# Summing a graph layer's messages by rounds of four blocks, with eleven picked tiles in each slot

## The chip, the core and the metric

The kernel runs on one core of a Trainium2 chip. The metric is the time of one execution on the device, in microseconds (us). TensorE is the matrix engine, VectorE, ScalarE and GpSimd the three others, SyncE issues most DMAs.

## What is computed

A graph of 12500 nodes with 16 values each and 400000 edges sorted by target, with 8 features each. After a normalisation and a ReLU come three layers of edge-conditioned convolution, then a product with a 16x16 matrix, and the result is added to x.

```python
def _nnconv(x, src, dst, edge_attr, ew, eb, rw, rb):
    W = (edge_attr @ ew + eb).reshape(edge_attr.shape[0], x.shape[1], rw.shape[1])
    xj = x[src]
    msg = jnp.einsum('ei,eio->eo', xj, W)
    agg = jax.ops.segment_sum(msg, dst, num_segments=x.shape[0])
    return agg + x @ rw + rb
# layers 1 and 2: h = relu(batchnorm(_nnconv(h, ...))); layer 3: relu(_nnconv(h, ...)) @ pred_w + pred_b
```

## The kernel before

**Tiling.** A tile is 128 edges, one in each partition. Five tiles make a block (640 edges that follow each other in the sorted order), five blocks a slot: 25 tiles, 3200 edges. A layer has G = 125 slots; five slots are a body, whose buffers turn (SLOTS). All three layers run the same code, so there are 375 slots.

**Getting x[src].** GpSimd fetches 15 of the 25 tiles of a slot from a table of the nodes in HBM, one indirect DMA for a tile (L469, `gather`). The other 10 are picked on chip. ScalarE makes one-hot matrices of the low nine bits of the source, as 4 x 128 rows, in two halves of five tiles: four `distance` (L915) and four `low_hot` (L921) in each half, from keys that SyncE loads as a broadcast (L396). TensorE multiplies each tile's one-hots with the node values, which are split in an upper and a lower part: 4 x 2 matmuls of 400 columns a tile (L1076, `pick`), into one of four PSUM banks. VectorE takes each bank with the mask of the upper bits (L684, `take_picks`), and after each half reduces its tiles to 16 values an edge (L689).

**Products and sums.** VectorE multiplies the 16 values with the 8 features (L639, once for the picked tiles and once for the fetched ones), ScalarE copies the 16 values beside them (L931, L937): 144 columns an edge, in one of three parts of `xbig`. TensorE sums them by target: `sum_tiles` (L1043) runs over j and then over the five blocks, and multiplies each tile with a one-hot of 32 targets (`hot`, L631, two buffers). Each block writes its own 32 partitions of PSUM, the column group n % 4, with n the number of the block. Four blocks form a round, so rounds don't end where slots do; a slot completes one round, every fourth slot two. ScalarE copies a completed round (`copy_rounds`, L879), TensorE transposes and merges it with a shifted one-hot (`transpose_round`, L1090, L1091), ScalarE copies that (L887, L888), and for each quad of four slots TensorE makes messages (`messages_of`, L1101, L1103), which VectorE adds into `agg` (`add_quad`, L725, five additions).

**Order.** Every engine has its own written order, joined by semaphores. TensorE, in slot g: the ten picks of slot g+1, with the transpositions of the rounds ended in slot g-1 after the second and the fourth and a quad's messages after the eighth, then the sum of slot g. VectorE, in slot g: products, round one-hots, feature copy for g+1 (L734), takes and reduction of the first half of g+1, target one-hots (L631), takes and reduction of the second half, masks for g+2 (L670), and, behind every fourth slot, the additions. ScalarE: the row copies, copies of the transposed rounds, then the two halves' one-hots of g+2, with the copy of the completed round between distances and one-hots of the second half. A tile may be picked once its bank was taken, four tiles before. A part of `xbig` is written again after slot k-3 is summed, a `hot` after k-2.

**Opening.** Sources of picked tiles come from HBM in two loads of ScalarE's queue (L838) into `key_all`, tiles across, 20 bytes a piece; VectorE splits them (L535 to L538), TensorE transposes the keys (L991), and ScalarE writes them to HBM (L850), from where the broadcasts read. The targets are loaded half by SyncE and half by ScalarE (L843). `rows` holds the node values of a layer in a tensor of its own, `rows_room`.

## Time and profile before

| what | value |
|---|---|
| median of 3 runs | 7477.99 us (7477.64 to 7480.97) |
| profiled execution: time, span | 7481.76 us, 7478.8 us |
| mean granted TensorE clock | 0.977 |
| busy: TensorE, VectorE, ScalarE, GpSimd | 7244.2, 5851.7, 4981.2, 5326.7 us |
| picking matmuls, L1076 | 30000 of 348 ns |
| gathers, L469 | 5625 of 947 ns |

The profile is one execution, recorded by the hardware. Busy time of an engine counts no waiting and no issuing. PE is TensorE's matmuls and PEld its weight loads, DVE VectorE, ACT ScalarE, POOL GpSimd, SP SyncE. Matmuls overlap, so the mean duration of one is longer than the distance from one to the next. "Idle before" is the time that the engine stood still ahead of an instruction, with what ended it.

### The profile page before, as it was taken

The page shows a single profiled execution, that of the slowest core. Times are in us where ns is not written, and L with a number is a line of the kernel's source. Part 1 is how long each engine was busy: PE and PEld are TensorE (multiplying, and loading weights), DVE is VectorE, ACT ScalarE, POOL GpSimd, SP SyncE. Part 2 cuts the span into 40 slices and gives each one's busy share as a digit, 9 for nine tenths or more (in the row PEclk, how much of TensorE's full clock was granted, in tenths as well). Part 3 has the DMA queues.
Part 4 walks back from the last instruction along what each step waited for, and adds up shares of the span by engine and source line. Part 5 has one row for each costly group of instructions (what it writes and reads, how often), then busy time and mean ns, then how long its engine had stood idle before and what let it go on. Part 6 is the DMA issues. An engine that isn't in the chain of part 4 may idle for free.

```text
span 7478.8 us, 138584 instructions
## 1 busy us (share of the span) xinstructions
PE 7244.2 (97%) x53192; PEld 6608.9 (88%) x53192; DVE 5851.7 (78%) x7566; ACT 4981.2 (67%) x8367; POOL 5326.7 (71%) x5635
## 2 busy tenths in 40 slices
PE   4999999999999999999999999999999999999998
PEld 1999999999999699999999999968999999999998
DVE  3888878787878678788888888867888888787885
ACT  3666666666666566666666666656666666666665
POOL 4677777777777377777777777737777777777772
PEclk7999999999999799999999999979999999999998
DMA  8111111111111111111111111111111111111110
GB/s 39 29 31 31 31 31 31 31 31 30 30 31 31 27 29 31 31 31 31 31 31 31 31 31 31 31 26 30 31 31 30 32 29 31 31 31 31 31 31 21
DMA packets 783276, 229.34 MB, mean 31 GB/s; under 512 B 643869, under 2 KB 733869, under 8 KB 782619
## 3 DMA queue, kind: packets, MB, share of 16 engines
q1 hardware_dynamic: 529252, 172.27, 11.0%
q0 software_dynamic: 180000, 46.44, 7.3%
q10 hardware_dynamic: 73367, 1.76, 1.0%
q8 instruction: 425, 6.96, 0.4%
q14 instruction: 232, 1.90, 0.1%
HBM read 216.52 MB, written 3.52 MB: 29 GB/s over the span
## 4 chain that ended last, share of the span: by engine, by line
PE 85%; DVE 7%; issue 4%; DVEq 3%; DMA 1%; ACT 0%; ACTq 0%
PE bank L1076 68%; PE bank L1043 10%; DVE xbig L639 3%; DVEq L720 3%; PE bank L1032 2%; PE bank L1091 1%; DVE agg L725 1%; DVE spread L684 1%; PE bank L1090 1%; PE bank L1101 1%; PE bank L1103 1%; DMA key_all<-in_src 1%; PE bank L1148 1%; PE bank L1160 1%; DVE xg L689 0%
## 5 line engine op out<-in xcount | busy, mean ns | idle before, releaser
L469 POOL DMA_INDIRECT xg<-node_table,idx x5625 | 5325.9, 947 | 2036.1 <-issue 1766.2
L1076 PE MATMUL bank<-nodes,low_hot 128*128 128x400 f32 x30000 | 5742.7, 348 | 68.9 <-DVE spread L684 52.2
L1076 PEld LDWEIGHTS bank<-nodes,low_hot 128*128 128x128 f32 x30000 | 5403.8, 188 | 279.0 <-issue 180.9
L915 ACT ACTIVATE distance<-key_all,low_id 128x640 bf16<-128x640 int16 x3000 | 2242.9, 818 | 1912.7 <-issue 1219.7
L684 DVE TENSOR_TENSOR spread<-mask,bank 128x400 f32<-128x400 uint8 x3750 | 1989.0, 564 | 1234.7 <-PE bank L1076 1234.5
L921 ACT ACTIVATE low_hot<-distance,one 128x640 fp32r<-128x640 bf16 x3000 | 2232.9, 817 | 0.0
L689 DVE TENSOR_REDUCE xg<-spread 128x80 f32<-128x2000 f32 x750 | 1677.0, 2236 | 25.7
L639 DVE TENSOR_TENSOR xbig<-xg,bank 128x1280 f32<-128x1280 f32 x750 | 1327.3, 1810 | 1.0 <-issue 0.2
L1043 PE MATMUL bank<-xbig,hot 128*32 128x144 f32 x18750 | 994.5, 295 | 0.0
L1043 PEld LDWEIGHTS bank<-xbig,hot 128*32 128x32 f32 x18750 | 820.6, 109 | 162.0 <-issue 99.1
L631 DVE TENSOR_TENSOR hot<-bank,dst_rel 128x800 f32<-128x800 f32 x375 | 367.8, 981 | 0.0
L887 ACT ACTIVATE zT<-bank 128x100 f32<-128x100 f32 x471 | 112.8, 239 | 225.5 <-PE bank L1091 223.7
L725 DVE TENSOR_TENSOR agg<-agg,bank 16x100 f32 x471 | 118.5, 252 | 140.2 <-issue 69.0
L1090 PEld LDWEIGHTS bank<-merge,z 128*128 128x128 f32 x942 | 167.2, 188 | 59.1 <-issue 54.9
L1090 PE MATMUL bank<-merge,z 128*128 128x100 f32 x942 | 177.0, 269 | 28.5 <-DVE agg L725 22.0
L931 ACT ACTIVATE xbig<-xg 128x160 f32<-128x160 f32 x375 | 126.6, 338 | 65.5 <-ACT low_hot L921 65.5
L1091 PE MATMUL bank<-merge,z 128*16 128x100 f32 x942 | 162.5, 254 | 0.0
L879 ACT ACTIVATE z<-bank 128x144 f32<-128x144 f32 x471 | 117.7, 270 | 58.2 <-PE bank L1043 58.2
L670 DVE TENSOR_TENSOR mask<-bank,fine 128x250 uint8<-128x250 f32 x375 | 153.6, 410 | 0.0
L937 ACT ACTIVATE xbig<-xg 128x240 f32<-128x240 f32 x375 | 145.6, 388 | 0.0
L714 DVE TENSOR_SCALAR merge<-bank,slide 128x100 f32<-128x100 f32 x471 | 139.0, 312 | 0.0
L734 DVE COPY bank<-ea 128x200 f32<-128x200 f32 x375 | 133.1, 355 | 0.3 <-DVE agg L593 0.2
(109 smaller groups left out, 998.6 us busy)
## 6 DMA issues: line engine op xcount, KB each, us to landing
key_all<-edge_keys SPq DMA_DIRECT2D x375, 320.0 KB, 3.7
xg<-node_table,idx POOLq DMA_INDIRECT x5625
ea<-in_edge_attr SPq DMA_DIRECT2D x375, 100.0 KB
idx<-in_src SPq DMA_DIRECT2D x375, 7.5 KB
node_table<-rows_room SPq DMA_DIRECT2D x3, 781.2 KB
xbig<-node_table SPq DMA_DIRECT2D x9, 192.0 KB
xbig<-in_x SPq DMA_DIRECT2D x2, 781.2 KB
xbig<-in_dst ACTq DMA_DIRECT2D x1, 782.5 KB, 67.4
```

The costliest lines, as they stand in the source:

```text
L469: pool.indirect_dma_start(out=xg[u][:, j, :], out_offset=None, in_=table[:, :], in_offset=bass.IndirectOffsetOnAxis(ap=idx[u][:, j:j + 1], ...
L631: return nc.vector.tensor_tensor(buf, p_col[:, 0:wide].unsqueeze(1).to_broadcast([P, tiles, wide]), rel.unsqueeze(2).to_broadcast([P, tile ...
L639: return nc.vector.tensor_tensor(buf[:, :, D:D + FD].rearrange("p j (f d) -> p j f d", d=D), xj, ef, ALU.mult)
L684: nc.vector.tensor_tensor(spread[:, t - t0, :, :], mask[k % PAIR][:, t, :].unsqueeze(1).to_broadcast([P, D, FINE]), p_sel[t % BANKS].rearr ...
L689: nc.vector.tensor_reduce(xg[u % SLOTS][:, FETCHED + t0:FETCHED + t1, :], spread[:, 0:t1 - t0, :, :], AX_X, ALU.add).then_inc(s_xg, 1)
L720: bases = [dve.value_load(base_i[0:1, r:r + 1], min_val=0, max_val=N - 1) for r in rounds]
L915: nc.scalar.activation(distance[f][:, 0:tiles.stop - tiles.start, :], key[u % KEYS][:, tiles, :], ACT.Abs, bias=low_id[:, f:f + 1]).then_i ...
L921: nc.scalar.activation(low_hot[:, f, tiles, :], distance[f][:, 0:tiles.stop - tiles.start, :], ACT.Relu, bias=one[:], scale=-1.0).then_inc ...
L1043: done = nc.tensor.matmul(p_z[n // GANG % PAIR][c * WIN:(c + 1) * WIN, :], onehots[:, t, :], buf[:, t, :], start=j == 0, stop=j == RUN - 1)
L1076: last = nc.tensor.matmul(p_sel[t % BANKS], low_hot[:, f, t, :], nodes[i][:, f, :, :].rearrange("p d f -> p (d f)"), start=(f, i) == (0, 1 ...
L1090: nc.tensor.matmul(p_zT, z[r % PAIR][:, D:D + FD], merge[r % SHIFTS][:], start=True, stop=True)
L1091: nc.tensor.matmul(p_zxT, z[r % PAIR][:, 0:D], merge[r % SHIFTS][:], start=True, stop=True).then_inc(s_T, 1)
```

## The change

`sum_tiles`, which summed the five blocks of a slot, becomes `sum_round`, which sums the four blocks of a round, for each round that a slot completes; a block left over is summed in the next slot's round, from the slot before's buffers. So `xbig` and `hot` are released by rounds (`slot_summed`), and there are three `hot` buffers. `rows_room` goes; `rows` lies in the third part of `xbig`. Every slot picks 11 tiles and fetches 14: the halves have five and six tiles, keys, one-hots, masks and `spread` grow accordingly, and the PSUM bank of a tile goes by a running count. The picked sources are loaded as one DMA of 125 contiguous rows of 1920 integers, one row a slot; keys are cut from them in place, and the upper bits are transposed instead. The diff, cut to its core:

```diff
-PICKED = 10
-FETCHED = TILES - PICKED
+MOST = 11
+FETCHED = 15
 FOLD = 4
 FOLD_BITS = 2
 BANKS = 4
 SLOTS = 5
 PAIR = 2
+HOTS = 3
...
-PARTS = (slice(0, 5), slice(5, 10))
-HALF = 5
+HALF = 6
...
-        rows_room = sb("rows_room", [P, PER * D])
-        rows = rows_room[0:NODE_P, :].rearrange("p (m d) -> p m d", d=D)
         xbig = sb("xbig", [P, TRIPLE * TILES * WIDTH])
+        rows_at = (TRIPLE - 1) * TILES * WIDTH
+        rows = xbig[0:NODE_P, rows_at:rows_at + PER * D].rearrange("p (m d) -> p m d", d=D)
...
-        hot = [sb(f"hot{i}", [P, TILES, WIN]) for i in range(PAIR)]
+        hot = [sb(f"hot{i}", [P, TILES, WIN]) for i in range(HOTS)]
...
+        src_c = xbig[0:G, src_at:src_at + LATER].bitcast(I32)
+        src_int = spread[0:G, :, :, :].rearrange("p a b c -> p (a b c)")[:, 0:LATER].bitcast(I32)
+        fine_f = spread[0:G, :, :, :].rearrange("p a b c -> p (a b c)")[:, 0:MOST * P].rearrange("g (c p) -> g c p", p=P)
...
+        def picks_of(g):
+
+            return MOST
+
+        def parts_of(g):
+
+            return slice(0, RUN), slice(RUN, picks_of(g))
+
+        def picks_to(k):
+
+            return MOST + sum(picks_of(h % G) for h in range(k))
+
+        def slot_summed(eng, k):
+
+            if k >= 0:
+                eng.wait_ge(s_round, k // G * R + rounds_done(k % G))
...
-                        for j in range(FETCHED):
+                        for j in range(TILES - picks_of(b * SLOTS + u)):
...
-            dve.wait_ge(s_src, 32)
-            step(nc.vector.tensor_scalar(src_int, src_pick, 7 + FOLD_BITS, None, ALU.logical_shift_right))
-            step(nc.vector.tensor_copy(fine[:].rearrange("p (g j) -> p g j", g=G), src_int))
-            step(nc.vector.tensor_scalar(src_int, src_pick, P * FOLD - 1, None, ALU.bitwise_and))
-            nc.vector.tensor_copy(key_f, src_int).then_inc(s_keyf, 1)
-            for c in range(PICKED):
-                dve.wait_ge(s_keyT, c + 1)
-                nc.vector.tensor_copy(key16[:, c, :], bank[c % 2][0:G, 0:P]).then_inc(s_key16, 1)
+            dve.wait_ge(s_src, 16)
+            step(nc.vector.tensor_scalar(src_int, src_c, P * FOLD - 1, None, ALU.bitwise_and))
+            for to, part in zip(picked_to(key16), picked_from(src_int)):
+                last = nc.vector.tensor_copy(to, part)
+            last.then_inc(s_key16, 1)
+            step(nc.vector.tensor_scalar(src_c, src_c, 7 + FOLD_BITS, None, ALU.logical_shift_right))
+            for to, part in zip(picked_to(fine_f), picked_from(src_c)):
+                last = nc.vector.tensor_copy(to, part)
+            last.then_inc(s_finef, 1)
+            fine_c = fine[:].rearrange("p (g c) -> p c g", c=MOST)
+            for c in range(MOST):
+                dve.wait_ge(s_fineT, c + 1)
+                nc.vector.tensor_copy(fine_c[:, c, :], bank[c % 2][:, 0:G]).then_inc(s_fine, 1)
...
-                dve.wait_ge(s_seg, k + CREDIT - 1)
+                slot_summed(dve, k - 2)
                 n = (b * SLOTS + u) * BLOCKS
-                onehots(hot[k % PAIR][:], dst_rel[:, n:n + BLOCKS, :].rearrange("p n j -> p (n j)")).then_inc(s_hot, 1)
+                onehots(hot[k % HOTS][:], dst_rel[:, n:n + BLOCKS, :].rearrange("p n j -> p (n j)")).then_inc(s_hot, 1)
...
             def take_picks(layer, b, u, half):
 
 
                 k = layer * G + b * SLOTS + u
-                t0, t1 = PARTS[half].start, PARTS[half].stop
+                g = b * SLOTS + u
+                t0, t1 = parts_of(g)[half].start, parts_of(g)[half].stop
+                done, at = picks_to(k), TILES - picks_of(g)
                 dve.wait_ge(s_mask, k + 1)
                 dve.wait_ge(s_xg, k * 2 + half)
                 for t in range(t0, t1):
-                    dve.wait_ge(s_pick, k * PICKED + t + (1 + PICKED))
+                    dve.wait_ge(s_pick, done + t + 1)
                     nc.vector.tensor_tensor(
                         spread[:, t - t0, :, :],
                         mask[k % PAIR][:, t, :].unsqueeze(1).to_broadcast([P, D, FINE]),
-                        p_sel[t % BANKS].rearrange("p (d f) -> p d f", d=D), ALU.mult).then_inc(s_taken, 1)
-                dve.wait_ge(s_taken, k * PICKED + (t1 + PICKED))
-                nc.vector.tensor_reduce(xg[u % SLOTS][:, FETCHED + t0:FETCHED + t1, :],
+                        p_sel[(done + t) % BANKS].rearrange("p (d f) -> p d f", d=D), ALU.mult).then_inc(s_taken, 1)
+                dve.wait_ge(s_taken, done + t1)
+                nc.vector.tensor_reduce(xg[u % SLOTS][:, at + t0:at + t1, :],
                                         spread[:, 0:t1 - t0, :, :], AX_X, ALU.add).then_inc(s_xg, 1)
...
-                dve.wait_ge(s_seg, k + CREDIT - 2)
-                products(xw[k % TRIPLE][:, TAKEN, :], xg[u][:, TAKEN, :], p_ea[k % PAIR][:, TAKEN, :])
+                slot_summed(dve, k - 2)
+                taken = slice(TILES - picks_of(b * SLOTS + u), TILES)
+                products(xw[k % TRIPLE][:, taken, :], xg[u][:, taken, :], p_ea[k % PAIR][:, taken, :])
...
-            for i in range(PICKED // RUN):
-                act.dma_start(src_pick[:, :, i * RUN:(i + 1) * RUN],
-                              src_b.rearrange("(g a) p j -> a p g j", a=BLOCKS)[FETCHED // RUN + i, :, :, :]
-                              ).then_inc(s_src, 16)
+            act.dma_start(src_c, src.rearrange("(g e) -> g e", g=G)[:, GE - LATER:GE]).then_inc(s_src, 16)
...
-                    act.wait_ge(s_key16, PICKED)
-                    act.dma_start(keys.rearrange("(c q) p -> q c p", q=G), key16).then_inc(s_keyd, 16)
+                    act.wait_ge(s_key16, 1)
+                    act.dma_start(keys.rearrange("(g c) p -> g c p", g=G), key16).then_inc(s_keyd, 16)
...
-                    act.wait_ge(s_seg, layer * G + g + (1 + CREDIT))
+                    act.wait_ge(s_round, n + 1)
...
-            def sum_tiles(g, buf, onehots):
-
-
+            def sum_round(layer, r):
+
+                n = layer * R + r
+                if n >= PAIR:
+                    pe.wait_ge(s_z, n - PAIR + 1)
+                blocks = range(r * GANG, min((r + 1) * GANG, NB))
                 for j in range(RUN):
-                    for a in range(BLOCKS):
-                        n, t = g * BLOCKS + a, a * RUN + j
-                        c = n % GANG
-                        done = nc.tensor.matmul(p_z[n // GANG % PAIR][c * WIN:(c + 1) * WIN, :], onehots[:, t, :],
-                                                buf[:, t, :], start=j == 0, stop=j == RUN - 1)
-                return done
+                    for i in blocks:
+                        k, t, c = layer * G + i // BLOCKS, i % BLOCKS * RUN + j, i % GANG
+                        last = nc.tensor.matmul(p_z[r % PAIR][c * WIN:(c + 1) * WIN, :], hot[k % HOTS][:, t, :],
+                                                xw[k % TRIPLE][:, t, :], start=j == 0, stop=j == RUN - 1)
+                last.then_inc(s_round, 1)
...
-                before = t - BANKS if t >= BANKS else max(range(t, PICKED, BANKS)) - PICKED
-                pe.wait_ge(s_taken, k * PICKED + (before + 1 + PICKED))
+                n = picks_to(k) + t
+                pe.wait_ge(s_taken, n - BANKS + 1)
                 for f in range(FOLD):
                     for i in (1, 0):
                         last = nc.tensor.matmul(
-                            p_sel[t % BANKS], low_hot[:, f, t, :],
+                            p_sel[n % BANKS], low_hot[:, f, t, :],
...
-                        behind = layer * R + ((g + 1) * BLOCKS - 1) // GANG - 1
-                        if behind > 0:
-                            pe.wait_ge(s_z, behind)
-                        sum_tiles(g, xw[k % TRIPLE], hot[k % PAIR]).then_inc(s_seg, 1)
+                        for r in rounds_of(g):
+                            sum_round(layer, r)
...
```

## Rows read from the trace of the kernel before

**Rows 1.** Page, part 1: busy us of each engine, share of the span, instructions.
```profile
PE 7244.2 (97%) x53192; PEld 6608.9 (88%) x53192; DVE 5851.7 (78%) x7566; ACT 4981.2 (67%) x8367; POOL 5326.7 (71%) x5635
```

**Rows 2.** Page, part 4: the chain that ended last, by line.
```profile
PE bank L1076 68%; PE bank L1043 10%; DVE xbig L639 3%; DVEq L720 3%; PE bank L1032 2%; PE bank L1091 1%; DVE agg L725 1%; DVE spread L684 1%; PE bank L1090 1%; PE bank L1101 1%; PE bank L1103 1%; DMA key_all<-in_src 1%; PE bank L1148 1%; PE bank L1160 1%; DVE xg L689 0%
```

**Rows 3.** Groups, whole run: line engine op out<-in shapes xcount | busy us, mean ns | idle before.
```profile
L1076 PE MATMUL bank<-nodes,low_hot 128*128 128x400 f32 x30000 | 5742.7, 348 | 68.9 <-DVE spread L684 52.2 <-DVE nodes L652 15.1 <-DVE agg L593 1.1
L469 POOL DMA_INDIRECT xg<-node_table,idx x5625 | 5325.9, 947 | 2036.1 <-issue 1766.2 <-DMA node_table<-rows_room 198.7 <-DMA ea<-in_edge_attr 71.2
...
L689 DVE TENSOR_REDUCE xg<-spread 128x80 f32<-128x2000 f32 x750 | 1677.0, 2236 | 25.7
L1043 PE MATMUL bank<-xbig,hot 128*32 128x144 f32 x18750 | 994.5, 295 | 0.0
```

**Rows 4.** Waits, whole run: engine line waited for: us in total, times, longest us.
```profile
PE bank L1076 <- DVE spread L684: 52.2, 92, 1.7
PE bank L1090 <- DVE agg L725: 22.0, 90, 0.6
...
POOL xg L469 <- issue: 1766.2, 5529, 77.2
```

**Rows 5.** Windows, a period of each kind: us, busy of each engine, PEclk, DMA, GB/s.
```profile
1334.45:1353.67 19.22, 18.50 (x135) 16.95 (x134) 15.99 (x23) 12.81 (x21) 14.35 (x17) 1.00 0.19 31
1353.67:1371.69 18.02, 18.02 (x136) 17.10 (x135) 14.81 (x18) 12.82 (x21) 13.28 (x15) 1.00 0.19 32
1371.69:1389.69 18.00, 18.00 (x135) 17.08 (x134) 15.05 (x19) 12.82 (x21) 13.74 (x15) 1.00 0.19 33
1389.69:1409.71 20.02, 20.02 (x159) 17.92 (x158) 14.81 (x18) 13.37 (x24) 15.15 (x17) 1.00 0.18 30
```

**Rows 6.** Timeline 1500:1525, kind 1: start us, us, engine line op out<-in xcount.
```profile
1504.50 2.64 PE L1043 MATMUL bank<-xbig,hot 128*32 128x144 f32 x50
...
1511.65 1.52 DVE L684 TENSOR_TENSOR spread<-mask,bank 128x400 f32<-128x400 uint8 x3
```

**Rows 7.** Timeline of TensorE, 1371.6:1390, kind 2.
```profile
1371.69 2.64 PE L1043 MATMUL bank<-xbig,hot 128*32 128x144 f32 x50
...
1377.27 0.36 PE L1090 MATMUL bank<-merge,z 128*128 128x100 f32 x2
...
1377.84 11.93 PE L1076 MATMUL bank<-nodes,low_hot 128*128 128x400 f32 x64
```

**Rows 8.** The same from 1371.6 to 1371.99: what of the sum had started.
```profile
1371.69 0.60 PE L1043 MATMUL bank<-xbig,hot 128*32 128x144 f32 x12
```

**Rows 9.** Timeline of VectorE, 1371.6:1390, kind 2.
```profile
1379.07 1.52 DVE L684 TENSOR_TENSOR spread<-mask,bank 128x400 f32<-128x400 uint8 x3
```

**Rows 10.** Timelines of VectorE and TensorE, 1334:1356, kind 0.
```profile
1338.45 1.79 DVE L725 TENSOR_TENSOR agg<-agg,bank 16x100 f32 x5 [0.72 <-issue]
...
1344.13 1.99 DVE L684 TENSOR_TENSOR spread<-mask,bank 128x400 f32<-128x400 uint8 x4
...
1340.38 0.43 PE L1090 MATMUL bank<-merge,z 128*128 128x100 f32 x2 [0.18 <-DVE agg L725]
...
1344.73 9.01 PE L1076 MATMUL bank<-nodes,low_hot 128*128 128x400 f32 x48 [0.54 <-DVE spread L684]
```

**Rows 11.** Timeline of ScalarE, 1334:1356, kind 0.
```profile
1334.61 2.98 ACT L915 ACTIVATE distance<-key_all,low_id 128x640 bf16<-128x640 int16 x4 [2.76 <-PE bank L1076]
1337.50 0.27 ACT L879 ACTIVATE z<-bank 128x144 f32<-128x144 f32 x1
```

**Rows 12.** The opening: timeline of VectorE, DMA of 0:95 (KB each, us to landing).
```profile
12.94 1.82 DVE L518 TENSOR_REDUCE ln_m<-xbig 125x100 f32<-125x1600 f32 x1 [7.80 <-DMA xbig<-in_x]
...
91.46 1.79 DVE L545 CAST xbig<-xbig 128x3125 f32<-128x3125 int32 x1 [34.00 <-DMA xbig<-in_dst]
...
DMA packets 132507, 5.63 MB, mean 59 GB/s; under 512 B 132083, under 2 KB 132256, under 8 KB 132506
...
key_all<-in_src ACTq DMA_DIRECT2D x2, 312.5 KB, 37.5
```

More of the change, by code:

```diff
@@ L62, in gnn_kernel @@
     assert E == G * GE and G == BODIES * SLOTS and FD == P and D * (F + 1) <= 512
[L63 removed]
+    assert GANG * WIN == P and QROUNDS * SPAN <= 512 and FETCHED % RUN == 0 and NB == BLOCKS * G
     assert N == NODE_P * PER and PER == CHUNKS * SUB and CHUNKS % SLOTS == 0 and CN <= 512
@@ L70, in gnn_kernel @@
     table = nc.dram_tensor("node_table", [N, D], F32, kind="Internal").ap()
-    keys = nc.dram_tensor("edge_keys", [G * PICKED, P], I16, kind="Internal").ap()
+    keys = nc.dram_tensor("edge_keys", [G * MOST, P], I16, kind="Internal").ap()
     def blocks_of(a, tail=""):
@@ L111, in gnn_kernel @@
         one = sb("one", [P, 1])
-        fine = sb("fine", [P, G * PICKED], U8)
-        mask = [sb(f"mask{i}", [P, PICKED, FINE], U8) for i in range(PAIR)]
+        fine = sb("fine", [P, G * MOST], U8)
+        mask = [sb(f"mask{i}", [P, MOST, FINE], U8) for i in range(PAIR)]
         spread = sb("spread", [P, HALF, D, FINE])
@@ L326, in landed @@
         def landed(eng, layer, g):
-            eng.wait_ge(s_gath[g % SLOTS], (layer * BODIES + g // SLOTS + 1) * 16 * FETCHED)
+            eng.wait_ge(s_gath[g % SLOTS], 16 * sum(TILES - picks_of(h % G) for h in
+                                                    range(g % SLOTS, layer * G + g + 1, SLOTS)))
         def ends_quad(g):
@@ L396, in load_keys @@
                 sp.dma_start(
-                    key[u % KEYS][:].rearrange("p t e -> p (t e)"),
-                    keys[bass.ds((b * SLOTS + u) * PICKED, PICKED), :].rearrange("(a t) e -> a (t e)", a=1)
-                    .to_broadcast([P, PICKED * P])).then_inc(s_key[u], 16)
+                    key[u % KEYS][:, 0:picks_of(g), :].rearrange("p t e -> p (t e)"),
+                    keys[(g + 1) * MOST - picks_of(g):(g + 1) * MOST, :].rearrange("(a t) e -> a (t e)", a=1)
+                    .to_broadcast([P, picks_of(g) * P])).then_inc(s_key[u], 16)
             AHEAD = 2
@@ L494, in _ @@
                 dve.sem_inc(s_low, 1)
-            for _ in range(PICKED):
+            for _ in range(MOST):
                 dve.sem_inc(s_taken, 1)
@@ L904, in compare_keys @@
                 k = layer * G + b * SLOTS + u
+                g = b * SLOTS + u
                 u = u % SLOTS
-                tiles = PARTS[half]
+                tiles = parts_of(g)[half]
                 act.wait_ge(s_key[u], body * 16 + 16)
-                act.wait_ge(s_pick, k * PICKED + tiles.stop)
+                if k:
+                    act.wait_ge(s_pick, picks_to(k - 1) + min(tiles.stop, picks_of((k - 1) % G)))
                 before = k * (4 * FOLD) + half * 2 * FOLD
@@ L978, in _ @@
         def _(pe):
-            for _ in range(PICKED):
+            for _ in range(MOST):
                 pe.sem_inc(s_pick, 1)
@@ L982, in _ @@
                 pe.sem_inc(s_root, 1)
-                pe.sem_inc(s_seg, 1)
             pe.wait_ge(s_ident, 1)
-            pe.wait_ge(s_keyf, 1)
-            flat = key_f.rearrange("p g j -> p (g j)")
-            for c in range(PICKED):
+            pe.wait_ge(s_finef, 1)
+            for c in range(MOST):
                 if c >= 2:
-                    pe.wait_ge(s_key16, c - 1)
-                nc.tensor.transpose(bank[c % 2][0:G, 0:P], flat[:, c * G:(c + 1) * G], ident[:]).then_inc(s_keyT, 1)
+                    pe.wait_ge(s_fine, c - 1)
+                nc.tensor.transpose(bank[c % 2][:, 0:G], fine_f[:, c, :], ident[0:G, 0:G]).then_inc(s_fineT, 1)
             def find_bases():
-                pe.wait_ge(s_key16, PICKED)
+                pe.wait_ge(s_fine, MOST)
                 pe.wait_ge(s_base, 1)
@@ L1067, in pick @@
                 k = layer * G + b * SLOTS + u
-                for half, tiles in enumerate(PARTS):
+                for half, tiles in enumerate(parts_of((b * SLOTS + u) % G)):
                     if t == tiles.start:
                         pe.wait_ge(s_low, k * 2 + (half + 1 + 2 * CREDIT))
-                before = t - BANKS if t >= BANKS else max(range(t, PICKED, BANKS)) - PICKED
-                pe.wait_ge(s_taken, k * PICKED + (before + 1 + PICKED))
+                n = picks_to(k) + t
+                pe.wait_ge(s_taken, n - BANKS + 1)
                 for f in range(FOLD):
@@ L1111, in segment_sums @@
                 apart(pe)
-                for t in range(PICKED):
+                for t in range(picks_of(0)):
                     pick(layer, 0, 0, t)
@@ L1118, in segment_sums @@
                         ended = list(rounds_of(g - 1)) if g else []
-                        for t in range(PICKED):
-                            if not (last and u == SLOTS - 1):
+                        for t in range(MOST):
+                            if not (last and u == SLOTS - 1) and t < picks_of(g + 1):
                                 pick(layer, b, u + 1, t)
```

55 lines of the change are left out of this document (32 added, 23 removed).

## The prediction

> **What bounds the kernel now.** I read the page's busy shares first: TensorE 97%, VectorE 78%, GpSimd 71%, ScalarE 67% [rows 1]. The chain that ended last agrees: 68% of it is the picking matmuls of L1076, 10% the sums of L1043 [rows 2]. GpSimd's 71% is too low, though. Each gather is 0.947 us of work and about 0.30 us of issue behind it: (5325.9 + 1766.2 - 77.2) / 5625 = 1.247 us each [rows 3, 4], so fifteen take 18.7 us. The loop's real period is in the windows, one for each kind of slot: 19.22, 18.02, 18.00 and 20.02 us, 75.26 us for four, 18.8 a slot [rows 5]. GpSimd and TensorE are therefore within 1% of each other. Which of them sets the pace? The waits decide it: TensorE has no wait for a gather, or for products made from gathered rows, only 52.2 us for VectorE's takes and 22.0 us for the additions into agg, about 90 of each [rows 4]. TensorE sets the pace and GpSimd keeps up just behind.
>
> Four kinds of slot repeat. With g the slot's number in the layer, kind 0 (g mod 4 = 0, 19.22 us) has VectorE's five additions into agg after its sum, kinds 1 and 2 have nothing special, kind 3 (20.02 us) is followed by two round transpositions and a quad's messages. By the diff, kind 3 will sum two rounds, the others one.
>
> **The eleventh picked tile on TensorE.** A tile is 8 matmuls of 400 columns. In an undisturbed stretch 64 of them take 11.93 us, with the last one's own 0.34 us: (11.93 - 0.34) / 63 = 0.184 us a matmul [rows 7], and over whole slots it comes to 0.182. So a tile costs 8 x 0.182 = 1.46 us, with nothing beside it on the engine: the windows show TensorE 18.00 of 18.00 us busy [rows 5]. 375 slots make +548 us.
>
> **Summing by rounds.** A slot's sum is 25 tiles of 2 matmuls (float32 takes two passes), five for each j, over four column groups; the fifth shares a group with the first. The 50 span 2.64 us, one of them 0.29: 2.35 us from first start to last [rows 3, 6]. If the doubled group makes a chain of 5 x 4 = 20 passes, one is 2.35 / 19 = 0.124 us. That there is such a chain, with the other groups beside it, shows at the start of a sum: 12 matmuls have started after 0.60 - 0.29 = 0.31 us [rows 8], three sets of four about 0.135 apart, where one by one at 0.124 would give three. A round has four blocks on four groups, so ten sets: 10 x 0.124 = 1.24 us at the chain's pace, 10 x 0.135 = 1.35 at the start's. I take 1.30, near the start's, since all four groups are busy there as in a round. A slot with one round then sums in 1.30 in place of 2.48 us, 1.18 less; kind 3 with two rounds takes 2.60, 0.12 more. Had TensorE been alone, a slot would be 1.46 - 1.18 = +0.28 in kinds 0 to 2 and +1.58 in kind 3, together +2.4 us for four.
>
> The Trainium skill (TensorEngine Tiling (Array Packing), Theoretical Speedup) gives up to fourfold speed where one operand dimension is 32 or less; by that bound a round would be 40 x 0.124 / 4 = 1.24 us, the lower of my two values. The row that shows 12 starts in 0.31 us agrees with concurrency, less with the full factor.
>
> **VectorE, which comes late.** What TensorE gives up in the sum it can use only if VectorE has taken a bank. The four PSUM banks let TensorE run four tiles into the next slot; the fifth waits for the first take. Between a slot's last take and that first take VectorE has the reduction of the half, the masks, two product instructions, the round one-hots and the feature copy. In a kind 1 slot the sum starts at 1504.50, the first take at 1511.65 [rows 6]; with 0.57 us for it the bank is free 7.72 us after the sum's start. In kind 2 (two round one-hots) it is 1379.07 + 0.57 - 1371.69 = 7.95 [rows 7, 9]. TensorE comes to its fifth tile at 1377.84 + 16 x 0.184 = 1380.8, 9.15 us after the start: slack 1.2 to 1.4 us today. In kind 0 the five additions stand between (1338.45, 1.79 us), the first take is at 1344.13, and TensorE's fifth tile starts at 1344.73, 0.54 us late; its transposition had waited 0.18 us and more before [rows 10]. So kind 0 is already timed by VectorE, 10.28 us after the sum's start.
>
> The change makes this stretch of VectorE longer: the second half has six tiles, so the reduction goes over 2400 elements for 2000. The 2000 take 2236 ns and the reduction of 1600 in the opening 1820 [rows 3, 12], so 400 elements are 0.42 us; I add 0.02 for the masks of eleven. The products stay 25 tiles in all. First takes end at 7.72 + 0.44 = 8.16 in kinds 1 and 3, 8.39 in kind 2, 10.67 in kind 0, and TensorE starts its fifth tile 0.05 us later (1344.13 + 0.57 = 1344.70 to 1344.73 in kind 0, rounded up). TensorE itself would be there at 9.15 - 1.18 = 7.97. After the fifth tile's start everything is as before and one tile more:
> - kind 0: 10.72 + (19.22 - 10.28) + 1.46 = 21.12, +1.90 us
> - kind 1: 8.21 + (18.02 - 9.15) + 1.46 = 18.54, +0.52
> - kind 2: 8.44 + (18.00 - 9.15) + 1.46 = 18.75, +0.75
> - kind 3: no wait, 20.02 + 1.46 + 0.12 = 21.60, +1.58
>
> The sum is +4.75 us for four slots, half of it stall. In kind 0 the stall stands first at the transposition behind the additions: TensorE comes there 1.18 us earlier, the additions end 0.42 later, so that wait grows from 0.2 or 0.3 to about 1.9 us.
>
> A layer has 123 periods with picks, 31 of each of kinds 0 to 2 and 30 of kind 3: 31 x (1.90 + 0.52 + 0.75) + 30 x 1.58 = 146 us, less 2 us because the first slot has no additions: 144, and 432 for three layers. The picks of slots 0 and 1, ahead of the first sum, add 2 x 1.46 and a stall of 0.4: +10 for three layers. The last period has no picks.
>
> **What is hidden.** GpSimd: 14 x 1.25 = 17.5 us in periods of 18.5 to 21.6; it idles, and nobody waits for it. ScalarE: eight operations a slot, half of them on six tiles; four of 640 elements take 2.98 us [rows 11], so a fifth more is at most 0.16 for each of four distances and four one-hots, 1.3 us in a slot where it has 6 idle [rows 5]. One deadline is close: the round's copy (L879) stands behind the half's four distances, at 1337.50, 3.05 us after the sum's start [rows 11]. It will end at 3.05 + 0.64 + 0.27 = 3.96 at most; TensorE wants it at 1377.27, which is 5.58 after its start [rows 7], less 1.18: 4.40. It fits, by 0.4 us. The third one-hot buffer replaces two, and hot and xbig are released one slot later, when slot k-2 is summed; TensorE sums that slot before it picks k's tiles, so VectorE and ScalarE, who wait for slot k's picks anyway, find the wait met. Behind it on VectorE would queue the products and on ScalarE the distances. SyncE's key load is a tenth larger and issued slots ahead; the gathers' release (slot k-5 summed) is as before.
>
> **The opening.** 32000 packets of 20 B (two loads, 312.5 KB, 37.5 us to land) become one load of 125 rows of 7.7 KB. The opening is bound by DMA: VectorE waits 34.0 us for in_dst at 91.46 us, and 132507 packets move in 95 us [rows 12]. Without 32000 of them, at the mean, 95 x 32000 / 132507 = 23 us less. Against this: the ScalarE half of in_dst is issued behind the square root, which needs in_x, landed at 12.94 us; the new load of 960 KB moves beside it. Doubling those 12 us would put its half of in_dst about 9 us later. Between -23 and 0 I take -15. Fine places now go through eleven transpositions of the same kind as the ten keys: nothing.
>
> The Trainium skill (DMA: Bandwidth & Descriptors, Why a DMA increments its semaphore by 16 and not by 1) says that a transfer goes over the largest number of engines up to 16 that divides its slowest dimension, which for 125 rows is 5. in_x, too, has 125 rows, and its landing at 12.94 us is the only row on it. By that rule the new load is slower than its size suggests, which speaks against a gain; the sum would lose its 15 us and be 7912.
>
> **The sum.** 7478.8 (span of the profiled execution) + 432 + 10 - 15 = 7906 us; that execution took 7481.8 by the clock of the runs and their median is 7478, 0.8 below the span. I round to **7900 us**, 5.6% above the median of the runs.
>
> **Rivals.**
> - *No new stalls* (the reduction is covered, VectorE is in time): +2.4 us x 92, +10, -15: 7695. Against it: kind 0 is at VectorE's limit already [rows 10]. Chance 0.07.
> - *Rounds are no faster for each tile* (instructions are issued no denser than 50 in 2.35 us, 0.047 each): one round 1.9, two 3.8 us. Kinds 1 and 2 +0.9, kind 0 +1.9, kind 3 +2.8: 6.5 x 92 = +600, 8075. For it: the mean pace of today's sums; against it: the 12 starts in 0.31 us [rows 8], 0.026 each. Chance 0.05.
> - *ScalarE comes late with the round's copy.* If its distances grow by more than the 0.4 us of slack, TensorE waits at the transposition; with 1 us it is some 0.8 us in kinds 1 and 2: 186 x 0.8 = +150, 8050. ScalarE's own idle time [rows 5] speaks against. Chance 0.07.
> - *The other side: GpSimd sets the pace after all.* 18.7 of 18.8 us is close enough that TensorE's 97% could be work stretched to fill. The place is L1076: a slot without stalls is 80 x 0.182 + 3.4, so 88 p + 2.3 after the change, and it decides in favour once the pitch p, no longer held back, falls under (17.5 - 2.3) / 88 = 0.173 us. The price is then GpSimd's fourteen gathers: 4 x 17.5 = 70 for 75.26, 5.3 x 92 = -485, near 6990. Against it: an engine that runs ahead is stopped at a wait, and no such wait is there [rows 4]; the granted clock is 1.00 [rows 5], the 2.4 GHz level. Chance 0.03.
>
> **Numbers.** My forecast has 0.78. Its own spread is 7850 to 7940: 10 either way from a round of 1.24 or 1.35 (only kind 3 feels it), 15 from the opening, and 20 for the stalls, differences of tenths that occur 280 times. With the ScalarE case in part, the range is 7800 to 7990; the no-stall case and the slow rounds stay outside. Faster by over 0.2% (about what a measurement of this kernel can tell) 0.03, same 0.01, slower 0.96.
>
> **What would show it.** L1076 at 33000 matmuls with its pitch unchanged; L1043's sums near 1.6 us in three slots of four and 2.9 in the fourth; TensorE waiting some 170 us for agg L725 and for the takes in three kinds of slot; windows of four slots near 80 us; gathers 5250, GpSimd idle; the reduction of the second half near 2.65 us. I am wrong if TensorE's waits for VectorE stay at 75 us, or if four slots take under 78.

## The result, and the profile after

The changed kernel takes 7886.5 us (median of 4 runs, 7883.3 to 7887.4) against 7479.3: 5.4% more, ratio 1.054 with a 95% interval of 1.053 to 1.056. The forecast was 7900. The profiled execution spans 7883.5 us.

The page of the changed kernel, part 1 and parts of 4 (share of the span in the chain that ended last) and 5 (groups: count | busy us, mean ns | idle before); they answer to [rows 1 to 3]:

```profile
PE 7518.8 (95%) x56193; PEld 6884.1 (87%) x56193; DVE 6222.7 (79%) x7944; ACT 5299.8 (67%) x8367; POOL 4970.8 (63%) x5260
...
PE 66%; DVE 23%; issue 7%; DVEq 3%; ACT 0%; DMA 0%; ACTq 0%
...
L1119 PE MATMUL bank<-nodes,low_hot 128*128 128x400 f32 x33000 | 6355.7, 349 | 102.8 <-DVE spread L725 79.1
L730 DVE TENSOR_REDUCE xg<-spread 128x80 f32<-128x2000 f32 x750 | 1833.9, 2445 | 25.7
L1086 PE MATMUL bank<-xbig,hot 128*32 128x144 f32 x18750 | 657.1, 288 | 0.7 <-DVE xbig L676 0.7
```

L1119 is the picking matmul, L1086 the sum. The picks are 3000 more at the same mean (349 ns for 348). The sums have the same count, but are busy for 657.1 us in place of 994.5. TensorE's share fell from 97 to 95% while the kernel got longer: it waits more, and 23% of the chain now runs through VectorE, for 7% before.

Who waited for whom (us in total, times, longest), and the windows of a slot of each kind, to be read beside [rows 4, 5]:

```profile
PE bank L1133 <- DVE agg L767: 130.0, 90, 1.8
PE bank L1119 <- DVE spread L725: 79.1, 179, 2.1
...
POOL xg L501 <- DMA ea<-in_edge_attr: 923.4, 332, 36.2
```

The last row is GpSimd standing still; nobody waits for its gathers.

```profile
1391.29:1411.98 20.69, 18.78 (x133) 17.39 (x132) 17.01 (x24) 13.66 (x21) 12.98 (x14) 1.00 0.17 30
1411.98:1430.61 18.63, 18.54 (x133) 17.46 (x133) 15.75 (x19) 13.67 (x21) 11.50 (x13) 1.00 0.18 32
1430.61:1449.46 18.85, 18.55 (x133) 17.46 (x132) 15.98 (x20) 13.67 (x21) 13.33 (x15) 1.00 0.19 32
1449.46:1470.97 21.51, 21.51 (x197) 19.57 (x197) 15.84 (x19) 14.22 (x24) 14.48 (x16) 1.00 0.17 29
```

These are kinds 0 to 3, 79.68 us together for 75.26 before. The granted clock is 1.00 in all of them, before and after. A layer from its first sum to its last is 2458.0 us for 2320.3 (first layer: 196.39 to 2654.40, before 206.16 to 2526.16), the other two layers are 2457.8 and 2457.6 for 2321.2 and 2320.4, so three are +412; the first sum comes 9.8 earlier. 412 - 10 = 402 of the 405 us between the spans.

### The profile page after: what moved, and what is told of

The parts are those of the page before. It is cut to its first block, busy times and chain, and to the rows that moved or that the text cites. A ratio compares the mean times of both kernels' runs of the same rounds, so it can differ in the third digit from the quotient of the medians.

```text
span 7883.5 us, 144582 instructions
## 1 busy us (share of the span) xinstructions
PE 7518.8 (95%) x56193; PEld 6884.1 (87%) x56193; DVE 6222.7 (79%) x7944; ACT 5299.8 (67%) x8367; POOL 4970.8 (63%) x5260
## 4 chain that ended last, share of the span: by engine, by line
PE 66%; DVE 23%; issue 7%; DVEq 3%; ACT 0%; DMA 0%; ACTq 0%
PE bank L1119 58%; DVE xbig L676 7%; DVE xg L730 7%; DVE spread L725 4%; PE bank L1086 3%; DVEq L762 2%; PE bank L1073 2%; DVE agg L767 1%; DVE merge L756 1%; DVE bank L776 1%; DVE mask L709 1%; PE bank L1134 1%; PE bank L1144 1%; PE bank L1146 1%; PE bank L1189 1%
## 5 line engine op out<-in xcount | busy, mean ns | idle before, releaser
L501 POOL DMA_INDIRECT xg<-node_table,idx x5250 | 4970.0, 947 | 2785.8 <-issue 1579.2
L1119 PE MATMUL bank<-nodes,low_hot 128*128 128x400 f32 x33000 | 6355.7, 349 | 102.8 <-DVE spread L725 79.1
L1119 PEld LDWEIGHTS bank<-nodes,low_hot 128*128 128x128 f32 x33000 | 5956.2, 188 | 373.4 <-DVE spread L725 193.0
L956 ACT ACTIVATE distance<-key_all,low_id 128x640 bf16<-128x640 int16 (+1 forms) x3000 | 2402.7, 871 | 2091.0 <-PE bank L1119 1223.7
L725 DVE TENSOR_TENSOR spread<-mask,bank 128x400 f32<-128x400 uint8 x4125 | 2189.9, 566 | 1330.3 <-PE bank L1119 1329.7
L962 ACT ACTIVATE low_hot<-distance,one 128x640 fp32r<-128x640 bf16 (+1 forms) x3000 | 2393.7, 872 | 0.0
L676 DVE TENSOR_TENSOR xbig<-xg,bank 128x1408 f32<-128x1408 f32 x750 | 1327.6, 1810 | 1.3 <-issue 0.5
L1086 PE MATMUL bank<-xbig,hot 128*32 128x144 f32 x18750 | 657.1, 288 | 0.7 <-DVE xbig L676 0.7
L1086 PEld LDWEIGHTS bank<-xbig,hot 128*32 128x32 f32 x18750 | 545.1, 110 | 101.0 <-issue 99.8
L973 ACT ACTIVATE xbig<-xg 128x176 f32<-128x176 f32 x375 | 131.7, 351 | 67.4 <-ACT low_hot L962 66.1
L709 DVE TENSOR_TENSOR mask<-bank,fine 128x275 uint8<-128x275 f32 x375 | 163.7, 437 | 0.0
```

Source lines behind the costliest of these rows:

```text
L501: pool.indirect_dma_start(out=xg[u][:, j, :], out_offset=None, in_=table[:, :], in_offset=bass.IndirectOffsetOnAxis(ap=idx[u][:, j:j + 1], ...
L676: return nc.vector.tensor_tensor(buf[:, :, D:D + FD].rearrange("p j (f d) -> p j f d", d=D), xj, ef, ALU.mult)
L709: nc.vector.tensor_tensor(mask[k % PAIR][:, 0:p, :], p_col[:, 0:FINE].unsqueeze(1).to_broadcast([P, p, FINE]), fine[:, (g + 1) * MOST - p: ...
L725: nc.vector.tensor_tensor(spread[:, t - t0, :, :], mask[k % PAIR][:, t, :].unsqueeze(1).to_broadcast([P, D, FINE]), p_sel[(done + t) % BAN ...
L956: nc.scalar.activation(distance[f][:, 0:tiles.stop - tiles.start, :], key[u % KEYS][:, tiles, :], ACT.Abs, bias=low_id[:, f:f + 1]).then_i ...
L962: nc.scalar.activation(low_hot[:, f, tiles, :], distance[f][:, 0:tiles.stop - tiles.start, :], ACT.Relu, bias=one[:], scale=-1.0).then_inc ...
```

## The experiments

Each kernel is the changed one with one edit, except where it says "before". Times are medians. Ratios are to the kernel before, from runs of it made beside each set of experiments (7479.7, 7480.9 and 7481.6 us), so differences across sets carry an error of some 2 us.

**The eleventh tile without the rounds.**

```diff
-                        for r in rounds_of(g):
-                            sum_round(layer, r)
+                        sum_slot(layer, g)      # the old order, then_inc(s_round, rounds ended)
```

> The changed kernel with its sums back in slots of five blocks: eleven picks, everything else as changed. Theory (TensorE natural pace or VectorE's first take, whichever is later): kinds 1 and 2 lose VectorE's stall and get the long sum, 18.01 + 1.46 = 19.5 us each, kind 3 21.5, kind 0 stays at VectorE's time, 20.7: 81.1 us for four slots against 79.7, 92 times +1.4, so 8015 us. Rival (the rounds are worth their whole 1.2 us in each slot, nothing of it lost in stalls): +3.6 us for four slots, 8215 us.

It took 8021.5 us (ratio 1.072, interval 1.070 to 1.074). Windows of kinds 0 and 1, then the waits:

```profile
1412.82:1433.51 20.69, 19.99 (x144) 18.43 (x143) 17.01 (x24) 13.67 (x21) 12.85 (x14) 1.00 0.16 29
1433.51:1453.00 19.49, 19.49 (x144) 18.57 (x143) 15.84 (x19) 13.67 (x21) 11.32 (x12) 1.00 0.18 30
...
PE bank L1120 <- DVE spread L725: 54.1, 93, 2.1
...
PE bank L1134 <- DVE agg L767: 21.0, 90, 0.5
```

Kind 0 is 20.69 us with either form of the sum: the reader sees a slot whose length VectorE sets. In kind 1 TensorE is busy throughout at 19.49. So beside eleven tiles the rounds are worth 8021.5 - 7886.5 = 135 us; 1.2 us in each of the 93 x 3 slots of kinds 0 to 2 would have been 335. The tile alone is 8021.5 - 7479.7 = 542 us, or about 555 with the shorter opening taken out.

**The rounds without the eleventh tile.**

```diff
         def picks_of(g):
-            return MOST
+            return MOST - 1
```

> The changed kernel with ten picked and fifteen fetched tiles: the rounds alone. TensorE would need 19.2 + 16.8 + 16.9 + 20.0 = 72.9 us for four slots, GpSimd's sixty gathers 74.9. Theory A (GpSimd becomes the pace at once, and TensorE ends a layer closer behind it, 25 us instead of 48): 7400 us, TensorE or VectorE waiting for gathers. Theory B (TensorE sets the pace, gathers hide): 7250 us.

It took 7325.6 us (0.979, 0.978 to 0.981): 2% faster than the kernel before, and between the two theories. VectorE's waits between 1000 and 1600 us, and between 6600 and 7250, late in the third layer:

```profile
DVE spread L725 <- PE bank L1119: 89.9, 107, 2.0
DVE agg L767 <- issue: 6.1, 8, 1.1
```

```profile
DVE spread L725 <- PE bank L1119: 90.5, 109, 2.0
DVE xbig L676 <- DMA xg<-node_table,idx: 19.7, 16, 2.3
```

In the middle of the first layer nobody waits for gathers; late in the third VectorE's products do. The period goes along: 18.25 us a slot over the first half of a layer, 18.7 to 18.8 over the last 40 slots with picks of the second and third. GpSimd's first gather of those two layers starts 73 us ahead of the first sum. The gathers of a slot are done 42 us before its products need them in slot 0, 15 us before in slot 40 and 1 to 2 us before in slot 80: the lead is spent at the difference between 18.74 and 18.25 us a slot, and gone after 72 to 80 slots. In the first layer, which starts with 84 us of lead and has 44 left at slot 10, it lasts for some 100. Theory A had forgotten this lead; theory B holds until it is spent. So where the additions stand last, the eleventh tile costs 7886.5 - 7325.6 = 561 us, and the rounds gave 154 us by themselves, with the opening.

**Who sets kind 0?** The five additions are left out inside the loop:

```diff
+            def skip_quad(layer, q):
+                dve.wait_ge(s_mm, layer * QUADS + q + 1)
+                for r in quad_rounds(q):
+                    dve.sem_inc(s_add, 1)
-                            add_quad(layer, (g - 1) // QUAD)
+                            skip_quad(layer, (g - 1) // QUAD)
```

> The changed kernel without VectorE's additions of a quad's messages into agg inside the loop (left out; only the last quad of a layer is added). Theory (a kind 0 slot is timed by VectorE, which has the additions between last and first take): kind 0 falls from 20.7 to kind 1's 18.6 us, 92 times -2.1: 7695 us, and TensorE's wait of 130 us for L767 is gone. Rival (kind 0's length is TensorE's own, one tile more): 7885 us.

It took 7686.9 us (1.028, 1.026 to 1.029). Windows of kinds 0 and 1:

```profile
1357.38:1376.00 18.62, 18.55 (x133) 17.46 (x132) 15.75 (x19) 13.67 (x21) 11.09 (x13) 1.00 0.17 31
1376.00:1394.63 18.63, 18.54 (x133) 17.46 (x133) 15.74 (x19) 13.67 (x21) 13.29 (x15) 1.00 0.17 33
```

Kind 0 has become kind 1. The additions, with the register loads that belong to them and go with them here, cost TensorE 2.07 us every fourth slot, 200 us in all: 1.79 of adding and 0.27 of standing still between VectorE's last take and its first.

**The additions elsewhere.** First only moved, ahead of the take of the tenth tile:

```diff
                 for t in range(t0, t1):
+                    if quad is not None and t == 9:
+                        add_quad(layer, quad)
```

> The changed kernel with the additions ahead of the take of the tenth tile, where VectorE waits 0.9 us for each tile. Theory: they start once the messages are there, and push the last takes back by 0.6 us instead of standing 2 us behind them: kind 0 from 20.7 to 19.2 us, 92 times -1.5: 7750 us. Rival (the additions wait for the messages and their register loads there, so that the last take comes 2 us late and nothing is gained): 7885 us.

It took 8047.2 us (1.076, 1.074 to 1.078): 161 slower, not 136 faster. The rival had the mechanism, but not the size. VectorE's timeline ahead of a kind 0 slot shows the first part of it:

```profile
1412.95 0.57 DVE L727 TENSOR_TENSOR spread<-mask,bank 128x400 f32<-128x400 uint8 x1 [2.00 <-PE bank L1121]
1416.23 1.79 DVE L769 TENSOR_TENSOR agg<-agg,bank 16x100 f32 x5 [2.71 <-issue]
1417.94 1.03 DVE L727 TENSOR_TENSOR spread<-mask,bank 128x400 f32<-128x400 uint8 x2
```

Ahead of the additions VectorE stands still for 2.71 us, by "issue", that is for nothing another engine does. It is its own queue, which loads five column numbers into registers. In the changed kernel those loads follow each other every 0.62 us from the start of the reduction, and the reduction and the masks run in the meantime:

```profile
L762 DVEq TENSOR_LOAD <-base_i x5: 298/301/313, 1392.0 to 1394.5; - x5
```

Moved behind a take that waits for TensorE, they have no cover. The second part shows on TensorE, in the kind 0 slot that follows and in its waits:

```profile
1415.75:1438.47 22.72, 20.11 (x133) 18.99 (x132) 17.48 (x25) 13.67 (x21) 14.71 (x16) 0.92 0.16 28
...
1426.51 12.04 PE L1121 MATMUL bank<-nodes,low_hot 128*128 128x400 f32 x56 [2.61 <-DVE spread L727]
...
PE bank L1121 <- DVE spread L727: 277.5, 187, 3.0
```

Kind 0 is 22.72 us for 20.69. The waits for VectorE grew by 277.5 - 130.0 - 79.1 = 68 us only. The other 95 us are TensorE's own: the same matmuls keep it busy for 7613.4 us in place of 7518.8. The 56 picks behind the wait of 2.61 us take 12.04 us for 10.49, and the granted clock in this slot is 0.92, where all windows shown above have 1.00; over the first 3.5 us behind the wait it is 0.56, near the lower of the two levels (1.2 and 2.4 GHz). The clock was granted low for a few microseconds some 80 times in the loops of this kernel and 8 times in those of the changed one, whose kind 0 waits 1.38 us, works, and waits 0.53. No run isolates what the clock follows; the rows show that it fell most often in the run whose TensorE stands still longest in one piece.

Then the loads issued early, behind the target one-hots, and the additions ahead of the last two takes:

```diff
+                            bases = None if quad is None else load_bases(quad)
-                            take_picks(layer, b, u + 1, 1)
+                            take_picks(layer, b, u + 1, 1, quad, bases)
```

> The changed kernel with the additions ahead of the last two takes of a half, and their five register loads of 0.62 us each behind the target one-hots, in the shadow of the first half's reduction. Theory (the additions ahead of a take cost 2.7 us of waiting for those loads, not the 1.8 of adding): the last take comes on time, kind 0 falls to kind 1's 18.6 us, 7700 us. Rival (the additions themselves are too long there): above 7886 us, as with the additions moved alone.

It took 7687.5 us (1.028, 1.026 to 1.029), 199 faster than the changed kernel and as fast as with no additions at all. The additions, and kind 0:

```profile
1357.00 1.78 DVE L772 TENSOR_TENSOR agg<-agg,bank 16x100 f32 x5
...
1359.32:1377.95 18.63, 18.56 (x135) 17.47 (x134) 15.74 (x19) 13.67 (x21) 11.20 (x13) 1.00 0.18 32
```

They start without a wait, and TensorE's waits for them are gone from the list. The additions stand at the same take as in the run before, and only the loads have moved: 2.7 us of register loads, and not 1.8 us of adding, were what failed to fit. With what followed on TensorE they cost 8047.2 - 7687.5 = 360 us.

**How long is VectorE's slack?** One comparison more in every slot, between the feature copy and the first take, its result unused; in the changed kernel and in the one before:

```diff
                 nc.vector.tensor_copy(p_ea[k % PAIR], ea[u][:]).then_inc(s_ea, 1)
+                nc.vector.tensor_tensor(junk[:], p_col[...], dst_rel[...], ALU.is_equal)
```

> The changed kernel with one comparison more on VectorE, 0.90 us, between the feature copy and the first take of every slot; nobody uses its result. Theory (VectorE's first take times kinds 0, 1 and 2, kind 3 has 1.5 us of slack): +0.90 in three of four slots, 92 times +2.7: 8135 us. Rival (only kind 0 is VectorE's): +85 us, 7970.

> The kernel before with the same comparison. Theory (slack of 1.4 and 1.2 us in kinds 1 and 2, 2.0 in kind 3, none in kind 0): only kind 0 grows, 92 times 0.90: 7563 us. Rival (the stretch is on the path in all kinds): 7815 us.

After: 8138.9 us (1.088, 1.086 to 1.090), before: 7563.3 us (1.011, 1.010 to 1.013). Windows of the four kinds after, then of kinds 0 and 1 before:

```profile
1430.65:1452.23 21.58, 18.77 (x133) 17.38 (x132) 17.90 (x25) 13.67 (x21) 13.70 (x15) 1.00 0.16 28
1452.23:1471.75 19.52, 18.54 (x133) 17.45 (x132) 16.64 (x20) 13.67 (x21) 11.32 (x12) 1.00 0.16 30
1471.75:1491.50 19.75, 18.55 (x133) 17.47 (x133) 16.87 (x21) 13.67 (x21) 13.22 (x14) 1.00 0.18 31
1491.50:1513.01 21.51, 21.51 (x198) 19.57 (x197) 16.64 (x20) 14.22 (x24) 14.04 (x15) 1.00 0.18 29
```

```profile
1349.78:1369.90 20.12, 18.50 (x135) 16.95 (x134) 16.89 (x24) 12.81 (x21) 15.11 (x16) 1.00 0.17 30
1369.90:1387.91 18.01, 18.01 (x135) 17.10 (x134) 15.63 (x19) 12.82 (x21) 13.01 (x14) 1.00 0.18 32
```

After, kinds 0, 1 and 2 grow by 0.89 to 0.90 us each and kind 3 not at all; before, kind 0 alone (kinds 2 and 3 are 18.01 and 20.02). The same 0.9 us costs 252 us in one kernel and 82 in the other. VectorE is busy for four fifths in both; its average says nothing of it.

**The opening.** The old loads of 20-byte pieces put back beside the new one:

```diff
+            for i in range(2):
+                act.dma_start(old[:, :, i * RUN:(i + 1) * RUN], ...).then_inc(s_src, 16)
-            dve.wait_ge(s_src, 16)
+            dve.wait_ge(s_src, 48)
```

> The changed kernel with the old two loads of 32000 pieces of 20 bytes put back in front (into a tensor that nobody reads before it is written again), beside the new load. Theory (the opening is bound by the number of packets): in_dst lands some 13 to 25 us later and the first sum moves with it, 7900 to 7910 us. Rival (the 10 us that the first sum came earlier is from the keys' path or the earlier square root): 7887 us.

It took 7909.4 us (median of 5, 7908.3 to 7910.6), 22.9 more than the changed kernel. Its first sum, and the changed kernel's, and what DMA moved in their first 95 us:

```profile
219.06 1.43 PE L1090 MATMUL bank<-xbig,hot 128*32 128x144 f32 x40
...
DMA packets 124763, 5.89 MB, mean 62 GB/s; under 512 B 124307, under 2 KB 124387, under 8 KB 124762
```

```profile
196.39 1.43 PE L1086 MATMUL bank<-xbig,hot 128*32 128x144 f32 x40
...
DMA packets 99883, 6.75 MB, mean 71 GB/s; under 512 B 98923, under 2 KB 99125, under 8 KB 99881
```

The first sum moves by 22.7 us, and the whole difference is there: in_dst is converted at 101.33 us in place of 78.70. The changed kernel moves more bytes in that time and fewer packets, and is earlier, so bytes don't set the pace. But the run doesn't show that the number of packets does. ScalarE's queue, here and then in the changed kernel:

```profile
24.00 21.22 ACTq L883 DMA_DIRECT2D xbig<-in_src  x1
...
45.31 0.39 ACTq L886 DMA_DIRECT2D xbig<-in_dst  x1
46.55 0.38 ACT L885 ACTIVATE ln_v<-ln_v,eps 125x100 f32<-125x100 f32 x1
```

```profile
25.50 0.38 ACT L881 ACTIVATE ln_v<-ln_v,eps 125x100 f32<-125x100 f32 x1 [22.85 <-DVE ln_v L557]
25.50 0.41 ACTq L882 DMA_DIRECT2D xbig<-in_dst  x1
```

Behind the old loads ScalarE's queue is held until 45 us, the square root (`ln_v`) comes 21 us later, and ScalarE's half of in_dst is issued at 45.31 in place of 25.50. That is 19.8 of the 22.6 us; from issue to landing the half takes 56.0 us for 53.2. The square root, which the rival named, moves in this run, and the run can't tell the two apart.

The kernel before can. There the square root stands at 25.29 and the half is issued at 24.07, about as in the changed kernel, and it takes 67.4 us to land. What the change gained is in those 67.4 - 53.2 = 14.2 us, with fewer packets beside it, and not in an earlier square root.

**A version that beats both.** Rounds, the loads early, and ten picked tiles everywhere or eleven in one slot of four:

```diff
-            return MOST
+            return MOST - 1                          # ten_loads_early
+            return MOST if g % 4 == 2 else MOST - 1  # mix_loads_early
```

> Rounds, ten picked tiles, the additions ahead of the last two takes with their register loads early. TensorE would need 16.8 + 16.8 + 16.9 + 20.0 = 70.5 us for four slots, 17.6 each; GpSimd's fifteen gathers are 18.74 us. Theory (GpSimd's head start of 72 us in each layer is used up after some 60 slots, then it sets the pace): near GpSimd's own 125 x 18.74 a layer, 7290 to 7325 us, the same as with ten picks and late additions or a little less. Rival (TensorE's pace alone counts): 7325 - 92 x 2.4 = 7105 us.

> The same with eleven picks in kind 2 alone, ten in the others. TensorE needs 72.1 us for four slots, 18.0 each, GpSimd 59 gathers, 73.7 us, 18.4 each. Theory (both sides near each other, GpSimd's head start covers most of the 0.4 us a slot): 7325 - 92 x 1.0 = 7230 us, faster than with ten everywhere. Rival (each eleventh tile costs its 1.46 us wherever it stands, gathers never count): 7105 + 92 x 1.5 = 7240 with ten everywhere faster still, at 7105.

Ten everywhere took 7326.5 us (0.979, 0.978 to 0.981), the same as without the early loads, though TensorE was given 2.4 us in every fourth slot. One in four took 7215.0 us (0.965, 0.963 to 0.966), 267 us faster than the kernel before. Four slots with ten everywhere, early and late in the first layer, and four with one in four:

```profile
473.87:544.51 70.64, 70.64 (x562) 66.25 (x561) 60.50 (x78) 51.81 (x87) 53.57 (x57) 1.00 0.20 33
1940.41:2015.35 74.94, 71.30 (x561) 66.11 (x561) 60.77 (x78) 51.84 (x87) 56.62 (x60) 1.00 0.19 31
```

```profile
1929.42:2002.04 72.62, 72.49 (x570) 67.62 (x569) 61.60 (x79) 52.65 (x87) 54.94 (x59) 1.00 0.19 32
```

Waits for gathers in the one and in the other:

```profile
DVE xbig L676 <- DMA xg<-node_table,idx: 295.7, 214, 3.5
```

```profile
DVE xbig L676 <- DMA xg<-node_table,idx: 18.3, 17, 2.3
```

There are both ends of the balance. With ten picks four slots take TensorE's 70.64 us as long as the lead lasts, and then 74.94, which is sixty gathers of 1.249 us. One gather less in four slots ends that for some 2 us: 1.46 for the tile, and the rest waits for VectorE. With the loads early an eleventh tile in every slot costs 7687.5 - 7326.5 = 361 us, and one in every fourth slot gains 112.

## Why the prediction was right, point by point

- *What bounds the kernel.* That GpSimd, a hundredth from TensorE's period, was not the pace was read from the missing waits. The gathers fell to 5250 and the kernel got slower, so for eleven tiles it holds. With ten tiles and faster sums GpSimd does come in, first by its head start and then fully: the rival was wrong for this change, and is right one step further on.
- *The eleventh tile.* 1.46 us each and 548 in all; 542 with the sums unchanged, the opening's gain in it. The pitch stayed (349 ns a matmul for 348). Right.
- *The rounds.* Taken as 1.30 us for 2.48. The trace after has 40 matmuls over 1.43 us; with one's own 0.29 taken off, 1.14 us from first start to last in ten sets. A set starts 0.123 us after the one before it, and only the first interval of a sum is longer, 0.147. A round is 1.25 us, nearer the chain's 1.24 than the 1.35 read from the first sets. From a sum's start to the pick behind it there are 1.36 us for 2.56 (1391.29 to 1392.65), 1.20 less where 1.18 was taken, and behind two rounds 2.59, 0.03 more where 0.12 was taken.
- *VectorE's stretch.* The reduction of 2400 took 2.65 us (1430:1441, kind 2), 0.42 more, as taken. First takes ended 8.17 us after the sum's start in kind 1 and 8.39 in kind 2, where 8.16 and 8.39 had been worked out. Kind 2:

```profile
1431.32 2.65 DVE L730 TENSOR_REDUCE xg<-spread 128x96 f32<-128x2400 f32 x1
...
1438.43 2.01 DVE L725 TENSOR_TENSOR spread<-mask,bank 128x400 f32<-128x400 uint8 x4
...
1439.05 10.48 PE L1119 MATMUL bank<-nodes,low_hot 128*128 128x400 f32 x56 [0.30 <-DVE spread L725]
```

  The fifth tile starts at 1439.05, 8.44 after 1430.61. Kinds 1 and 2 were still 0.09 and 0.10 us longer than predicted. From there to the next sum it is 10.41 us (1449.46), where 8.85 + 1.46 = 10.31 had been taken from a slot without a wait. The missing 0.1 us is at the first pick behind the wait: the second starts 0.29 us after it, the others 0.18 after each other. The same 0.29 stands behind the transposition at 1435.28, where TensorE didn't wait, so it is the price of a break in the row of picks, and the wait made one break more. That was not in the sum.
- *Kind 0 is the term that was mis-sized most*: 20.69 us, predicted 21.12. The step was "the additions end 0.42 later" with the reduction. They did not. They start 4.0 us after the sum's start in both kernels, [rows 10] before and here:

```profile
1391.29 1.43 PE L1086 MATMUL bank<-xbig,hot 128*32 128x144 f32 x40
...
1395.28 1.79 DVE L767 TENSOR_TENSOR agg<-agg,bank 16x100 f32 x5 [0.27 <-issue]
```

  Before, they had stood 0.72 us behind "issue", which the row showed and the prediction passed over: the register loads, not the reduction, come last there (in both kernels the additions start 3.3 us after the first load, at 1335.2 before and 1392.0 here). Now 0.27 is left of the gap, and the reduction's 0.42 went into it; TensorE's fifth tile starts 10.27 us after the sum's start, for 10.28 before. It made the forecast 0.43 x 92 = 40 us too long; the 0.1 us behind waits in two kinds made it 18 too short, and kind 3, 0.09 shorter than predicted by its two rounds, another 8 too long. By spans: 7906 before rounding, less 30, is 7876, and 7883.5 was measured. Two of the 7 us left lie ahead of the first sum. The rest is covered by eight slots of kind 0 that took 21.5 to 21.8 us in place of 20.69, some 9 us in all. In each the clock was granted low for a few microseconds; the first of them:

```profile
1071.04:1092.84 21.80, 20.07 (x134) 19.01 (x133) 17.09 (x24) 13.66 (x21) 14.28 (x16) 0.92 0.17 28
```

  That the total came within 14 us is in part luck: terms that were 40 and 8 us too long stand against terms of 18 and 9 that were too short or missing.
- *TensorE's wait behind the additions* was to be some 170 us; it is 130.0, with 22.0 before, since the additions end no later.
- *The opening*: -15 taken from between -23 and 0. in_dst was converted at 78.70 us in place of 91.46, 12.8 earlier. The size is right, the reasons only in part. That fewer packets let in_dst land sooner fits (67.4 us from issue to landing before, 53.2 now). The cost set against it did not come: in_x did land later beside the new load, at 17.83 us in place of 12.94, but in the kernel before the square root had not waited for in_x. ScalarE's queue was held by the second old load until 24.00, and the square root stood at 25.29; now it stands at 25.50. The 22.9 us with the packets put back equal the upper bound by coincidence, since 19.8 of them are the later issue.

```profile
17.83 1.82 DVE L550 TENSOR_REDUCE ln_m<-xbig 125x100 f32<-125x1600 f32 x1 [12.60 <-DMA xbig<-in_x]
...
78.70 1.79 DVE L582 CAST xbig<-xbig 128x3125 f32<-128x3125 int32 x1 [37.27 <-DMA xbig<-in_dst]
```

  The Trainium skill's rule on 125 rows (DMA: Bandwidth & Descriptors, Why a DMA increments its semaphore by 16 and not by 1: they go over 5 engines) would fit a slower in_x beside another load of 125 rows; the gain that it was to cost came all the same. No run here tells its share. Without the gain the prediction's sum is 7478.8 + 432 + 10 = 7921 us, and not the 7912 given there.
- *ScalarE* stayed in time: in the windows of the four kinds TensorE has no wait for the round's copy.

## What to carry to other kernels

Work out each kind of iteration by itself, as a race between two engines to one instruction, with the slack of each; a saving on the bounding engine is worth only that slack, here 135 us of 335. When two engines are within a few per cent, split the work in smaller steps than one item for every iteration: with the register loads early, one tile in four slots gained 112 us where one in every slot cost 361. "Issue" ahead of an instruction can be a queue's own work with a price of its own, and it needs cover from work queued ahead of it. And a wait can cost more than its length: 95 of the 161 us lost with the additions moved were TensorE working at a lower clock behind its waits.

## What the runs showed of the hardware

A register load on VectorE's queue takes 0.62 us, and five of them beside the reduction and the masks left 0.27 us of standstill; behind a take that waited they left 2.71. Four column groups ran float32 passes of 144 columns side by side, four every 0.123 us, which is the pace worked out for a single chain (0.124). Behind a wait, as behind a transposition, the second pick starts 0.29 us after the first in place of 0.18. Where TensorE had stood still for 2.61 us, the granted clock was 0.56 over the next 3.5 us and 56 picks took 12.04 us for 10.49. An engine that issues loads of many small pieces is held by them: ScalarE's queue was held for 22.8 us by the second of two loads of 16000 pieces of 20 bytes, and for 21 us by the load issued next, whether its pieces were large or small.
